# Graph attention stage: VectorE's statistics and scaling moved ahead of the next step's one-hot matrices and messages

## The reference

```python
alpha = jnp.einsum('ehf,hf->eh', m, att)
amax = jax.ops.segment_max(alpha, dst, num_segments=n)
ex = jnp.exp(alpha - amax[dst])
denom = jax.ops.segment_sum(ex, dst, num_segments=n)
alpha = ex / (denom[dst] + SM_EPS)
out = jax.ops.segment_sum(x_l[src] * alpha[..., None], dst, num_segments=n)
out = out.mean(axis=1) + bias
mu = out.mean(axis=0)
var = out.var(axis=0)
out = gamma * (out - mu) * jax.lax.rsqrt(var + BN_EPS) + beta
```

## Time and profile before

| what | value |
|---|---|
| runs (median, lowest, highest) | 4888.35, 4884.67, 4892.93 us |
| profiled execution, own time | 4895.64 us |
| its span | 4894.1 us |
| mean granted TensorE clock over the span | 0.848 |
| busy share of the span: PE, DVE, ACT, POOL | 77%, 68%, 43%, 62% |
| attention stage, first to last instruction of VectorE in it | 2401.7 to 3127.7 us |

### The profile page before, as it was taken

The page is one execution under the profiler, slowest core; times in us unless marked ns, Lnnn a source line. Parts: engine busy times, 40 slices in busy tenths (PEclk is TensorE's granted clock), DMA queues, the critical chain, the costliest instruction groups (busy, mean ns, idle before and its releaser), DMA issues. The chain is left out here.

```text
span 4894.1 us, 87037 instructions
## 1 busy us (share of the span) xinstructions
PE 3752.4 (77%) x26626; PEld 3401.5 (70%) x26626; DVE 3316.4 (68%) x9195; ACT 2123.6 (43%) x5278; POOL 3043.4 (62%) x3590
## 2 busy tenths in 40 slices
PE   5720477758888799999288888896888688868888
PEld 5720477757878688887166666695888688868888
DVE  8978577757777677777699999883444344435544
ACT  6836244434444455555266666562222122212222
POOL 0001677747775677776377777446777577757775
PEclk9965677768888899999699999757898888878898
DMA  8013577757776566565232323365666466646665
GB/s 216 20 28 80 129 186 186 182 130 154 161 159 144 131 142 144 142 144 118 39 62 57 63 57 63 71 155 114 137 135 135 102 136 136 136 103 133 135 134 112
DMA packets 1661080, 588.72 MB, mean 120 GB/s; under 512 B 1564647, under 2 KB 1591078, under 8 KB 1660394
## 3 DMA queue, kind: packets, MB, share of 16 engines
q1 hardware_dynamic: 941766, 305.00, 27.3%
q10 hardware_dynamic: 636612, 195.74, 17.0%
q0 software_dynamic: 82272, 82.81, 8.6%
HBM read 387.27 MB, written 209.21 MB: 122 GB/s over the span
## 5 line engine op out<-in xcount | busy, mean ns | idle before, releaser
L2005 POOL DMA_INDIRECT early<-node_g,src_w x1173 | 1113.5, 949 | 426.2 <-issue 356.7
L2222 POOL DMA_INDIRECT early<-node_g,src_w x782 | 761.7, 974 | 295.2 <-issue 248.2
L2689 POOL TENSOR_SCALAR faS<-node_id,edge_id 128x128 f32<-128x128 f32 x560 | 373.8, 690 | 164.4 <-POOLq L1290 94.8
L1122 POOL DMA_INDIRECT fscat<-node_g,early x392 | 371.1, 947 | 164.2 <-issue 116.1
L2266 PE MATMUL bank<-l0S,l0msg 128*128 128x128 f32 x1568 | 279.1, 360 | 159.0 <-issue 83.5
L1223 ACT ACTIVATE fslz<-bank 128x264 f32<-128x264 f32 x784 | 304.9, 392 | 200.6 <-PE bank L1174 152.0
L2266 PEld LDWEIGHTS bank<-l0S,l0msg 128*128 128x128 f32 x1568 | 269.6, 271 | 165.4 <-issue 142.0
L2581 PEld LDWEIGHTS bank<-early,faS 128*128 128x128 f32 x1568 | 302.5, 196 | 93.8 <-issue 53.1
L2581 PE MATMUL bank<-early,faS 128*128 128x256 f32 x1568 | 365.7, 392 | 0.0
L1276 DVE TENSOR_TENSOR fslz<-fslz,bank 128x1848 f32<-128x1848 f32 x112 | 232.8, 2079 | 149.5 <-ACT fslz L1223 142.2
L2787 DVE SCALAR_TENSOR_TENSOR faagg<-bank,early,famine 128x64 f32<-128x64 f32 x1568 | 306.2, 275 | 18.6 <-issue 11.4
(11 more groups left out here) (401 smaller groups left out, 10350.9 us busy)
## 6 DMA issues: line engine op xcount, KB each, us to landing
edge_h<-early SPq DMA_DIRECT2D x280, 224.0 KB
node_g<-amax ACTq DMA_DIRECT2D x224, 224.0 KB
early<-edge_h SPq DMA_DIRECT2D x168, 256.0 KB
early<-node_g,src_w POOLq DMA_INDIRECT x1955
l0msg<-edge_a ACTq DMA_DIRECT2D x56, 256.0 KB
l0msg<-edge_h SPq DMA_DIRECT2D x56, 256.0 KB
l1msg<-edge_h SPq DMA_DIRECT2D x56, 256.0 KB
early<-dst_rows SPq DMA_DIRECT2D x56, 256.0 KB
```

What stands on the lines that cost most here:

```text
L1122: pool.indirect_dma_start(out=cat[:, s, t, lo:lo + F], out_offset=None, in_=node_g, in_offset=bass.IndirectOffsetOnAxis(ap=src_i[:, col], ...
L2005: pool.indirect_dma_start(out=ring[:, n % RING, t, :], out_offset=None, in_=table_in, in_offset=bass.IndirectOffsetOnAxis(ap=src_w[:, n * ...
L2222: pool.indirect_dma_start(out=ring[:, n % RING, t, :], out_offset=None, in_=table_in, in_offset=bass.IndirectOffsetOnAxis(ap=src_w[:, n * ...
L2689: ins = g.tensor_scalar(S[:, s, k, :], node_id[:, :], edge_id[:, at:at + 1], None, ALU.is_equal)
```

## The change

In the loop over the steps on VectorE, `moments(n - 2)`, the drain and `scale(n)` come first, and `first_matrices(n + 1)` and `messages(n + 1)` after them. `differences(n + 1)` and `weights(n + 1)` stay at the end. No instruction is added or removed, no other engine's list changes, and no semaphore or its count changes.

```diff
--- before.py
+++ after.py
@@ -2793,14 +2793,13 @@
                     differences(0)
                     weights(0)
                     for n in range(NS):
+                        if n >= 2:
+                            moments(n - 2)
+                        v.drain()
+                        scale(n)
                         if n + 1 < NS:
                             first_matrices(n + 1)
                             messages(n + 1)
-                        if n >= 2:
-                            moments(n - 2)
-                        v.drain()
-                        scale(n)
-                        if n + 1 < NS:
                             differences(n + 1)
                             weights(n + 1)
                     moments(NS - 2)
```

More of the change, by code:

```diff
@@ L2795, in _ @@
                     for n in range(NS):
-                        if n + 1 < NS:
-                            first_matrices(n + 1)
-                            messages(n + 1)
                         if n >= 2:
@@ L2803, in _ @@
                         if n + 1 < NS:
+                            first_matrices(n + 1)
+                            messages(n + 1)
                             differences(n + 1)
```

## The result

| | median us | runs |
|---|---|---|
| before | 4887.67 | 4884.67 to 4892.93 |
| after | 5037.19 | 5036.73 to 5038.55 |
| ratio | 1.0299 | 95% interval 1.0286 to 1.0312 |

A forecast was written before the change was run, and what follows sets the result against it. VectorE's list, 12.7 us a step, was taken as the bound. The new step was 13.7 us at full clock plus 1.5 for a slow TensorE stretch, 15.14 with one in 25 spared: +131 us over 55 steps, 5020 us, range 4932 to 5067.

The forecast's parts named there:

- VectorE's list was the bound, and the order hid the waits: VectorE, 92% busy, sets the 12.75 us step; matrices and messages cover ScalarE's and TensorE's work before scaling.
- Scaling behind the weights, +0.87 us: VectorE's statistics and scaling, right behind the weights, take 7.15 us instead of 6.28, waiting for ScalarE's tiles.
- Messages at 2.2 us: VectorE's messages fall from 3.49 to 2.2 us, as GpSimd's `own_rest` no longer starts ahead; a gain of 1.28.
- Small sums 3.09 us behind `halves`, a wait of 1.0: Before differences, VectorE waits 1.0 us for TensorE's small sums, which end 3.09 us after ScalarE's `halves` start.
- Who is late next: ScalarE's `outputs`, behind TensorE's last matmuls, delay the next `own_edges`; 13.7 us a step at full clock.
- The sign it gave: If right, L2764 or L2787 on VectorE waits for ScalarE about 2 us a step.
- The clock: TensorE, idle 3.2 us a step, then runs slow: 1.5 us a step, one step in 25 spared; clock about 0.88.
- two of the 25: Idle times in the old trace with transposes and sums both slow, 2.8 and 2.9 us more in all.
- GpSimd's list, costed at nothing: GpSimd's 9.4 us of busy time a step fits the longer step; its tiles are ready before scaling needs them.
- Full clock: Rival: TensorE stays at full clock or its slow stretches cost nothing; 13.7 us a step, +52 us, 4940; chance 0.20.
- Two whole stretches in every step: Rival: TensorE's transposes, outputs and next sums all slow; 16.5 us a step, +206 us, 5094; chance 0.14.
- the faster rival: Rival: messages take 2.2 us and nothing else waits; VectorE's list 11.47 us, -71 us, 4818; chance 0.04.

The follow-up runs named there:

- sums_first: own_first with TensorE's outputs(n - 2) moved behind sums(n), ahead of the transposes; 4951.04 us, ratio 1.0112.
- before_swap: The kernel before, with messages(n + 1) put ahead of first_matrices(n + 1) and nothing else moved; 4897.67 us, ratio 1.0008.
- stats_between: The kernel before, with moments(n - 2) put between first_matrices(n + 1) and messages(n + 1); 4866.16 us, ratio 0.9948.
- after_fill: The changed kernel with five extra matmuls in TensorE's idle time ahead of the last transposes; 4961.98 us, ratio 1.0137.
- own_first: The changed kernel with ScalarE's own_edges(n + 1) ahead of outputs(n - 1) and VectorE's moments(n - 2) behind the messages; 5037.99 us, ratio 1.0298.
- only_messages: The kernel before with only messages(n + 1) moved behind scale(n), first_matrices(n + 1) staying ahead of it; 4850.29 us, ratio 0.9906.

## Why the prediction was right

By its own steps, in its order.

*VectorE's list was the bound, and the order hid the waits.* Right: with the same instructions, and shorter messages at that, VectorE's share fell from 92% to 73%.

*Scaling behind the weights, +0.87 us.* The size is right where nothing else is late: from the weights' end to the next matrices it is 7.07 us in sums_first (2754.30 to 2761.37), as in the earlier trace rows (3117.98 to 3125.05). The last step of the old trace was a true sample of the new order.

*Messages at 2.2 us.* 2.28. The reason given, `own_rest` starting first, was shown twice, by before_swap, where the stall moved to the matrices, and by stats_between, where it shrank with the overlap. A pure swap of the two instructions would have been forecast wrongly (I did, in its expectation): only an order that puts something else beside `own_rest` gains.

*Small sums 3.09 us behind `halves`, a wait of 1.0.* It was 1.40 in the steps with slow transposes and 1.03 in after_fill, at full clock.

*Who is late next.* The size was right, 13.7 us, measured to the hundredth in after_fill, but the step named one waiter where there are two. `outputs` on ScalarE ahead of `own_edges` and `outputs` on TensorE ahead of the sums come out at the same time; I put only the first on the path. own_first took the first away and won nothing; sums_first took both away and won 87 us (TensorE's order alone was not moved, so whether it needs ScalarE's too is open). That they tie is seen in after_fill: `own_edges` starts at 2751.70, and by the earlier trace rows its first tile is there 1.17 us later, at 2752.87; scaling starts at 2753.00 behind the first bank. The prediction had not worked out when that bank comes at full clock, so that the 13.7 us held with half of the cause missing was luck. The sign it gave, L2764 or L2787 waiting about 2 us a step for ScalarE, came half true: L2764 waits 1.1 us for ScalarE, L2787 0.8 us for TensorE. The bound is TensorE's loop: matrices, `halves`, last transposes, small sums, `outputs`, sums, scaling.

*The clock.* Right in kind: 3.29 us idle (3.2 forecast), each step slow. The term was under-sized: 1.5 us a step, against 15.36 (mean of 14.82 and 15.90) - 13.70 = 1.66 us, and no step was spared where one in 25 was allowed. It had priced a stretch that begins in `outputs`. Here the last transposes are slow already (0.90 us) in all but the first steps: from their start to that of `outputs` it is 1.47 us (2762.39 to 2763.86) against 1.25 in after_fill (2748.07 to 2749.32). With `outputs` 0.90 us longer (2.62 against 1.72) that makes 1.12 us, the step of 14.82. In every second step `outputs` are 1.53 us longer and the sums 0.44, which makes 2.19, the step of 15.90. The trace of before had more warning than the prediction read from it: "two of the 25" should have been three (at 2764.84, 3034.28 and 3085.80 the transposes take 0.90 us and the sums 7.1 to 7.3). That more work falls into the slow stretch fits the clock of 0.83, where 0.88 was forecast. Of the 17 us between 5020 and 5037, 9 are this term ((15.30 - 15.14) x 55); the rest is about the slower profiled execution of before that the sum was made against.

*GpSimd's list, costed at nothing.* Right, though its matrices became slower: 836 ns each in the groups of after, 679 in those of before (2440 to 3105 us). `own_rest` still takes 1.47 us and ends at 2769.08, and the waits view of after has no wait of scaling for GpSimd.

*The rivals.* Full clock did not happen by itself, and when it was forced the kernel was 68 us over the one before (4961.98 - 4894.06), against 52 forecast; 9 of the 16 us between are the steps over 13.70 us (mean 13.87). Two whole stretches in every step did not happen, but the 15.9 us steps are part of the way. The shorter messages, the mechanism of the faster rival, are real, and only_messages is the order that keeps them and pays little for it (0.26 us a step in scaling).

## What to carry to other kernels

When an in-order engine is the bound, each early instruction in its list may be what starts a long chain on the other engines; look for the chain that ends back at this engine and keep its first link early (the matrices), and move what nobody waits for long (the messages). Halve a reordering before dropping it: of two moves that together cost 3.0%, one alone was worth -0.9% and the other +3.4%. A trace often has the new order somewhere already, in its first or last step, where there is no next step to overlap; its rows price the waits better than sums of durations do.

## What the runs showed of the hardware that I had not expected

The stall between VectorE and GpSimd goes to whoever comes second, and then on: in before_swap GpSimd's multiply, held off by the messages for 1.9 us (3.39 against 1.47), went ahead of VectorE's next instruction with two SBUF inputs and lengthened it from 0.68 to 1.96 us, so exchanging the two won nothing. The Trainium skill (SBUF — State Buffer, "SBUF: two separate sides") describes an exclusive lock held for a whole instruction; the trace agrees, and adds that VectorE, with its next instruction queued up, did not get it again before GpSimd. And a higher TensorE clock is worth only what waits behind TensorE: 0.93 to 1.00 brought nothing in the kernel before, 0.83 to 0.99 brought 75 us in the changed one, and 0.92 to 1.00 nothing in sums_first.
